# Attention and a routed feed-forward layer on one core: the routing's eight columns beside the values' 256, in one product

## The reference

```
xn = layernorm(x)                                  # each token's 256 features
q, k, v = xn @ Wq.T + bq, xn @ Wk.T + bk, xn @ Wv.T + bv
attn = softmax((q * 16**-0.5) @ k.T per head) @ v  # 16 heads of 16
attn = attn @ Wo.T + bo

inh  = sigmoid(xn @ Wr / temperature)              # Wr is 256 x 8: the routing
dist = abs(inh - 1/e)
w    = exp(-dist/0.1) where LOWER <= inh <= 0.5    # if none of the 8: the top 2 of exp(-dist/0.3)
w    = w / sum(w)
h_e  = silu(xn @ Wg[e]) * (xn @ Wu[e])             # 8 experts, 256 inner features each
ffn  = sum_e w[e] * (h_e @ Wd[e])

out  = x + attn + ffn
```

## Time and profile before

| | us |
|---|---|
| median of 3 runs (lowest, highest) | 6346.64 (6344.07, 6350.4) |
| the profiled execution | 6347.73 |
| its span, first to last instruction | 6346.0 |
| TensorE busy | 6238.5 |
| VectorE busy | 5524.7 |
| ScalarE busy | 4809.4 |
| GpSimd busy | 512.8 |

### The profile page before, as it was taken

How to read it: one execution, slowest core, us unless ns; L and a number is a source line. 1 busy time by engine, 2 the same in 40 slices (tenths; PEclk the granted TensorE clock), 3 DMA queues, 4 the chain that set the end, 5 groups by cost and what they waited for, 6 DMA issues and landing times. The chain is left out here.

```text
span 6346.0 us, 123466 instructions
## 1 busy us (share of the span) xinstructions
PE 6238.5 (98%) x48776; PEld 3210.4 (51%) x48776; DVE 5524.7 (87%) x8211; ACT 4809.4 (76%) x9045; POOL 512.8 (8%) x535
## 2 busy tenths in 40 slices
PE   7999999989999999999999999999999999999998
PEld 6888888863444444444444444444444444444444
DVE  4545555559999999999999999999999999999992
ACT  3333333316888888888888889898888898888886
POOL 1222222220000000000000000000000000000000
PEclk9999999988999999999999999999999999999999
DMA  2111111121111111111111111111111111111213
GB/s 97 41 45 47 41 47 47 40 43 23 30 30 30 30 30 30 35 35 33 35 35 31 30 30 31 30 30 30 30 30 30 30 30 34 35 35 34 37 51 127
DMA packets 243329, 244.98 MB, mean 39 GB/s; under 512 B 159473, under 2 KB 204273, under 8 KB 236401
## 3 DMA queue, kind: packets, MB, share of 16 engines
q1 hardware_dynamic: 231720, 206.04, 15.0%
q0 software_dynamic: 11024, 30.94, 2.1%
HBM read 159.26 MB, written 76.58 MB: 37 GB/s over the span
## 5 line engine op out<-in xcount | busy, mean ns | idle before, releaser
L966 DVE TENSOR_REDUCE mx<-sc 128x1 f32<-128x512 f32 (+1 forms) x6144 | 4782.8, 846 | 10.5 <-PE sc L839 10.1
L946 ACT ACTIVATE pr<-st 128x512 f32<-128x512 f32 x8120 | 4265.7, 603 | 480.2 <-PE st L852 475.7
L839 PE MATMUL sc<-experts 48*128 48x512 f32 x8192 | 2826.6, 447 | 24.1 <-DVE mx L966 15.2
L852 PE MATMUL st<-experts 50*128 50x512 f32 x8120 | 2699.1, 432 | 0.1
L860 PE MATMUL pv<-pr,vst 128*32 128x256 f32 (+1 forms) x24440 | 2396.9, 464 | 1.9 <-ACT pr L946 0.9
L852 PEld LDWEIGHTS st<-experts 50*128 50x128 f32 x8120 | 1306.3, 184 | 1828.4 <-ACT pr L946 1652.3
L839 PEld LDWEIGHTS sc<-experts 48*128 48x128 f32 x8192 | 1330.6, 186 | 98.4 <-DVE mx L966 80.8
L860 PEld LDWEIGHTS pv<-pr,vst 128*32 128x32 f32 x24440 | 481.6, 108 | 956.6 <-issue 915.7
L433 ACT ACTIVATE gated<-gate 128x512 f32<-128x512 f32 x256 | 152.2, 599 | 634.4 <-PE up L76 634.2
L603 DVE TENSOR_TENSOR hraw<-gated,up 128x512 f32<-128x512 f32 x256 | 173.1, 685 | 433.8 <-ACT gated L433 430.7
L76 PE MATMUL gate<-xT,experts 128*128 128x512 f32 x1536 | 408.2, 402 | 11.5 <-issue 11.5
(11 more groups left out here) (106 smaller groups left out, 1329.8 us busy)
## 6 DMA issues: line engine op xcount, KB each, us to landing
experts<-parts_d SPq DMA_DIRECT2D x372, 256.0 KB, 4.4
parts_d<-part SPq DMA_DIRECT2D x64, 512.0 KB, 3.0
x_in<-in_L_attn_hidden_states SPq DMA_DIRECT2D x16, 512.0 KB, 4.6
v_d<-v_sb SPq DMA_DIRECT2D x32, 256.0 KB, 2.2
vst<-v_d SPq DMA_DIRECT2D x128, 64.0 KB, 2.2
sums_d<-oT SPq DMA_DIRECT2D x256, 32.0 KB
whole<-sums_d POOLq DMA_DIRECT2D x32, 256.0 KB, 2.9
recs<-rden_d POOLq DMA_DIRECT2D x32, 256.0 KB, 5.7
```

The source lines that it names most:

```text
L839: nc.tensor.matmul(sc_bank(g % RINGB), qr[par][r0:r0 + TERMS, q0:q0 + P], kr[par][r0:r0 + TERMS, b * GT:(b + 1) * GT], start=True, stop=Tr ...
L852: nc.tensor.matmul(score_bank(at, x), kr[par][r0:r0 + ROWSM, kb * P:(kb + 1) * P], qr[par][r0:r0 + ROWSM, q0:q0 + GT], start=True, stop=Tr ...
L946: nc.scalar.activation(pr[:, (QSUB * kb + j) % PRING, :], score_bank(2 * at + q, x), ACT.Exp).then_inc(st_read, 1)
L966: nc.vector.reduce_max(mx[par][:, t, i:i + 1], sc_bank(first, n), AX.X).then_inc(sc_read, 1)
```

## The change

The routing's weights `Wr` no longer have a tensor of their own. They stand behind the 256 columns of the values' weights, so `wT[2]` has VR = 264 columns. The units `route` and `v` are replaced by four units `v`, one for each tile of 128 tokens: 8 matmuls of 264 columns, with low x low for all columns. The values lie in columns 0 to 255 of the bank, the routing in 256 to 263. VectorE does two instructions for each of the four, the addition of the values' bias and the scaling of 8 columns into `rt`. Behind the fourth it goes on with the same chain as before. The order of units is now x, v, q, k, and the table is

```
-MISC = (("x", 0), ("x", 1), ("route", 0), ("q", 0), ("q", 1), ("k", 0), ("k", 1), ("v", 0), ("v", 1))
-MISC_AFTER = {1: (0, 1), 2: (2,), 3: (3, 4), 5: (5, 6), 7: (7, 8)}
+MISC = (("x", 0), ("x", 1), ("v", 0), ("v", 1), ("v", 2), ("v", 3), ("q", 0), ("q", 1), ("k", 0), ("k", 1))
+MISC_AFTER = {1: (0, 1), 2: (2, 3), 3: (4, 5), 5: (6, 7), 7: (8, 9)}
+VR = D + E
```

On TensorE:

```
+            def values_and_routes(bank, x):
+
+                terms = [(k, hx, hw) for k in range(KC) for hx, hw in ((0, 0), (0, 1), (1, 0), (1, 1))]
+                for n, (k, hx, hw) in enumerate(terms):
+                    last = nc.tensor.matmul(bank[:, 0:VR], x[k][hx], c.wT[2][hw][:, k, :], start=(n == 0), stop=(n == len(terms) - 1))
+                return last
+
-                elif kind == "route":
-                    pe.wait_ge(misc_free, g * len(MISC) + KC)
-                    for t in range(TPG):
-                        last = product(nc, bank[:, t * E:(t + 1) * E], tile_of(xT[par], t), pieces(c.wr), low_low=True)
...
-                    for j in range(2):
-                        last = product(nc, bank[:, j * D:(j + 1) * D], tile_of(xT[par], 2 * i + j), pieces(c.wT[2]))
+                    if i == 0:
+                        pe.wait_ge(misc_free, g * len(MISC) + KC)
+                    last = values_and_routes(bank, tile_of(xT[par], i))
```

On VectorE (the instruction at L512 goes from the head of `route`, and so does the old part of `v`), and on ScalarE, where the three exponentials belong to the fourth `v`:

```
+                elif kind == "v":
+                    dve.wait_ge(misc_full, g * len(MISC) + n + 1)
+                    bank = misc[(par * len(MISC) + n) % 2]
+                    if i % 2 == 0:
+                        dve.wait_ge(v_stored[i // 2], (g + 1) * DMA)
+                    nc.vector.tensor_tensor(v_sb[i // 2][:, i % 2, :], bank[:, 0:D], c.bv[:, :], ALU.add)
+                    nc.vector.tensor_scalar(rt[:, 0, i, :], bank[:, D:VR], c.rtemp[:, 0:1], None, ALU.mult).then_inc(misc_free, 1)
+                    if i < TPG - 1:
+                        return
+                    w, rtotal, over, link, count = route(g, par)
...
-                if kind == "route":
+                if kind == "v" and i < TPG - 1:
+                    return
+                if kind == "v":
```

SyncE stores the values ahead of the parts, and waits for each by the new numbers of units:

```
-                    wait_alone(sp, misc_free, g * len(MISC) + KC + 1 + u + 1, passed)
+                    wait_alone(sp, misc_free, g * len(MISC) + KC + TPG + u + 1, passed)
...
-                    wait_alone(sp, misc_free, g * len(MISC) + len(MISC) - 1 + i, passed)
+                    wait_alone(sp, misc_free, g * len(MISC) + KC + 2 * i + 2, passed)
...
                 if not last:
+                    store_v(g + 1)
                     store_parts(g + 1)
-                    store_v(g + 1)
```

More of the change, by code:

```diff
@@ L68, in wait_alone, with product @@
     engine.sem_inc(passed, 1)
-def product(nc, out, lhs, rhs, low_low=False):
-    terms = [(a, b) for k in range(len(lhs)) for a, b in ((0, 0), (0, 1), (1, 0)) + (((1, 1),) if low_low else ())]
-    terms = [(k, a, b) for k in range(len(lhs)) for a, b in terms[:len(terms) // len(lhs)]]
+def product(nc, out, lhs, rhs):
+    terms = [(k, a, b) for k in range(len(lhs)) for a, b in ((0, 0), (0, 1), (1, 0))]
     for n, (k, a, b) in enumerate(terms):
@@ L172, in _ @@
                 act.wait_ge(s_t, u + 1)
-                nc.scalar.activation(c.wT[u // KC][0][:, u % KC, :], psT[u % 2][:, 0:D], ACT.Identity,
+                nc.scalar.activation(c.wT[u // KC][0][:, u % KC, 0:D], psT[u % 2][:, 0:D], ACT.Identity,
                                      scale=SCALE if u < KC else 1.0).then_inc(s_high, 1)
@@ L185, in _ @@
                     dve.wait_ge(s_high, u + 1)
-                    nc.vector.scalar_tensor_tensor(out=c.wT[n][1][:, i, :], in0=psT[u % 2][:, 0:D], scalar=SCALE if n == 0 else 1.0,
-                                                   in1=c.wT[n][0][:, i, :].bitcast(F32), op0=ALU.mult, op1=ALU.subtract).then_inc(s_low, 1)
+                    nc.vector.scalar_tensor_tensor(out=c.wT[n][1][:, i, 0:D], in0=psT[u % 2][:, 0:D], scalar=SCALE if n == 0 else 1.0,
+                                                   in1=c.wT[n][0][:, i, 0:D].bitcast(F32), op0=ALU.mult, op1=ALU.subtract).then_inc(s_low, 1)
             dve.wait_ge(s_id, 1)
@@ L192, in _ @@
             nc.vector.reciprocal(c.rtemp[:, :], temp[:, :]).then_inc(s_const, 1)
-            nc.vector.tensor_copy(c.wr[0][:, :, :], wr[:, :, :]).then_inc(s_const, 1)
+            nc.vector.tensor_copy(c.wT[2][0][:, :, D:VR], wr[:, :, :]).then_inc(s_const, 1)
             dve.wait_ge(s_const, 4)
-            nc.vector.tensor_tensor(c.wr[1][:, :, :], wr[:, :, :], c.wr[0][:, :, :], ALU.subtract).then_inc(s_const, 1)
+            nc.vector.tensor_tensor(c.wT[2][1][:, :, D:VR], wr[:, :, :], c.wT[2][0][:, :, D:VR], ALU.subtract).then_inc(s_const, 1)
             for n in range(3):
@@ L303, in before @@
                 load(1, 1)
+                store_v(0)
                 store_parts(0)
-                store_v(0)
             def body(g, par, last, more):
@@ L410, in misc_unit @@
                     nc.scalar.activation(rt[:, 7, :, :], rt[:, 5, :, :], ACT.Exp, scale=-1.0 / 0.3).then_inc(exp_given, 1)
-                    return
-                if kind == "v":
                     return
@@ L494, in norm, with route @@
                 ins.then_inc(xn_done, 1)
-            def route(g, par, n):
+            def route(g, par):
                 count = [2]
@@ L508, in over @@
                     return v.unsqueeze(2).broadcast_to([P, TPG, E])
[L510 to L513, removed]
                 dve.wait_ge(exp_given, g * 3 + 1)
@@ L559, in misc_unit @@
                                             ALU.subtract).then_inc(misc_free, 1)
-                elif kind == "route":
-                    w, rtotal, over, link, count = route(g, par, n)
+                elif kind == "v":
[8 more added lines that the diff above has]
+                    w, rtotal, over, link, count = route(g, par)
                     link(nc.vector.reciprocal(rs[:, 0, :], rtotal))
@@ L570, in misc_unit @@
                                                    in1=part[u % 2][:, 0, :].bitcast(F32), op0=ALU.add, op1=ALU.subtract).then_inc(misc_free, 1)
[L571 to L576, removed]
             def add_expert(g, par, e):
@@ L1160, in layer @@
             c.experts = [sb(f"experts{hl}", [P, 3, E, KC, FI], F32R) for hl in range(2)]
-            c.wT = [[sb(f"wT{n}{hl}", [P, KC, D], F32R) for hl in range(2)] for n in range(3)] + [c.woT]
-            c.wr = [sb(f"wr{hl}", [P, KC, E], F32R) for hl in range(2)]
+            c.wT = [[sb(f"wT{n}{hl}", [P, KC, VR if n == 2 else D], F32R) for hl in range(2)] for n in range(3)] + [c.woT]
             c.before = sb("before", [P, E, E], F32)
```

## The result

| | before | with the change |
|---|---|---|
| median of 4 runs, us | 6345.35 | 6306.4 (6304.17 to 6308.68) |
| ratio, 95% interval | | 0.9936 [0.9924, 0.9948] |
| span of the profiled execution, us | 6346.0 | 6306.0 |
| opening, first transpose to first gate product | 27.68 | 23.65 |
| token loop, first gate to last down product | 1303.94 | 1264.89 |

What follows compares the result with a forecast made beforehand. TensorE was taken to bound the token stage. The sum -37.5 - 27.2 + 17.2 - 3.8 = -51.3 us gave 6295 us as a median; own range 6287 to 6304, range of 8 in 10 6279 to 6320.

Steps and rivals of the forecast that it cites:

- rival B: Token loop, TensorE's wait for `hraw`: the clock still falls there, 15 falls of 1.6 us, 6319 us; chance 0.18.
- The array: TensorE's matmuls per group: narrow routing and 256-column values out, 32 of 264 columns in at 123.3 ns; 37.5 us won.
- The clock: Token loop, behind the routings: TensorE's clock no longer falls to its lower level; all 27.2 us won, bounds 0 and 27.2.
- The wait: Gate product after expert 4: TensorE waits 1.15 us for VectorE's `hraw`, 17.2 us lost in 15 groups.
- The addition: VectorE ahead of the routing's chain: a 128x256 bias addition takes 0.41 us; with the shorter scaling, 0.38 us more.
- Rival A: Token loop, gate product after expert 4: no wait for `hraw` appears, 6278 us; chance 0.12.
- C: The 512 matmuls of 264 columns: eight columns cost their own pass, 229 ns each, clock falls stay, 6376 us; chance 0.05.
- The opening: Ahead of the token loop: values and routing first, first gate product at about 68.5 not 72.36; 3.8 us won.
- one or two falls of the clock more or less at the loop's turn: TensorE's pauses where the loop branches back: a part of the forecast's own range, 6287 to 6304 us.
- the k stores: Behind expert 7, stores of the moved k units: base store issued some 1 us later, all of it hidden.
- The attention stage: Behind the token stage: same program before and after, costed at nothing; a move over a few us would refute.

## Why the prediction was right, and where 12 us went

The measured 6306.4 lies inside the range of 8 in 10, 6279 to 6320, but 2 us outside the 6287 to 6304 that the forecast gave itself. The upper end was set for rival B, a clock that falls at the wait, which didn't happen; that it also covered a cost that nobody had seen is luck. Term by term:

The array: forecast 37.5 us. Measured 3.87 us for two pairs of value units and not 3.95, so 3.49 + 2.87 + 0.09 - 3.87 = 2.58 a group, 38.7. Right.

The clock: forecast 27.2. It falls nowhere in the changed loop, and the two falls at the turn (3.2) are gone too: 30.4. The first part is shown to come from the narrow matmuls. The second isn't the change's: over the ten other profiles the clock fell behind two turns in three, behind one in three and behind none in four.

The wait: forecast 1.15 us of path in 15 groups, 17.2. TensorE could have gone on at 669.23 + 2.87 = 672.10 and did at 673.18: 1.08. The idle times of the 15 waits add up to 14.7 us, and what the down products ahead of them take longer from start to start adds up to 17. The addition takes 0.42 and the scaling 0.22, as worked out. Rival A falls, and so does B: the clock did not fall behind a single wait. C falls: 264 columns cost 121 ns and not 229.

The opening: forecast 3.8, measured 4.03. The value units there:

```profile
48.69 5.71 PE L344 MATMUL misc<-wT,xT 128*128 128x264 f32 x32 [1.50 <-DVE xT L558]
54.24 2.91 PE L75 MATMUL misc<-xT,wT 128*128 128x512 f32 x12
63.58 5.49 PE L75 MATMUL misc<-xT,wT 128*128 128x512 f32 x12 [6.43 <-DVE part L577]
68.87 1.75 PE L75 MATMUL gate<-xT,experts 128*128 128x512 f32 x6
```

5.55 us where 5.5 was worked out, and the gate at 68.87 where 68.5 was.

What failed is a term that the sum did not have. The prediction took the pauses at the loop's turn as they were ("one or two falls of the clock more or less at the loop's turn") and asked only what the clock did behind them. They grew from 11.5 to 21.1 us of idle time, which makes TensorE some 10.6 us later. Two things made them: the opening got 48 instructions shorter, which put an edge of a block 25 instructions (256 - 231) behind the loop's head, and the k stores, twice the size of the values', moved to the turn. The prediction had looked at these stores only for who waits for them by a semaphore, and at the code not at all.

A small one: a product behind a pause takes 5.61 us and not 5.46 (673.18 to 678.79), which in 15 waits and 6 new starts is 3 us. The loop then: -38.7 - 30.4 + 17 + 10.6 + 3 = -38.5, measured -39.05. The attention stage is 2.6 us longer, but over the eleven profiles of this study it ran from 4960.2 to 4966.0 with the same instructions, so nothing shows an effect of the change. The setup ahead of the first transpose, 0.5 us longer, ran from 44.2 to 46.2 us in them.

## What to carry to other kernels

A unit that gives the array almost nothing to do can cost half of its own time again by the clock (27.2 us beside 15 x 3.49): fill it or join it to a wide one. When units are put in another order, each wait has to be read again from what now covers it, since here both orders left one uncovered. And a rolled loop has a price at its turn that depends on where its code lies and on what DMAs run then; look for pauses that nothing released and for packets of the instruction queue beside them, give the branch its hint, and count the blocks that the loop touches.

## What was not expected of the hardware

- Taking 24 matmuls away ahead of a loop, and moving stores to its turn, added a pause of 1.2 to 1.5 us at each of six turns. A hint took 21.1 us of pauses down to 1.1.
- With the hint and the head at slot 23, the loop of 1880 instructions was not loaded again at its turns: 13 packets of the instruction queue in the loop, not 73.
- 264 columns cost 121 ns, hardly more than 256 (120) and 8 (109), and 512 cost 227 to 229. Between 256 and 264 the eight columns were nearly free.
- The clock's falls behind the same routings cost 27.2, 22.4 and 28.8 us in the three profiles that have them, of three kernels whose routings are the same.
